# A four-stage convolution kernel: the image loop written out, and the copies of the normalised image dealt to two DMA queues

## The reference

```python
x = x + L0(_gn(x))   # Winograd convolution, tiles of 6 x 6 giving 4 x 4
x = x + L1(_gn(x))   # 3 x 3 convolution to 18 offsets, prelu, then a deformable 3 x 3 convolution:
                     # bilinear samples at the moved places, 8 groups
x = x + L2(_gn(x))   # four 3 x 3 convolutions with binarised weights, quantised activations between
x = x + L3(_gn(x))   # 3 x 3 convolution, |vertical difference| through a 1 x 1, channel attention
```

## Time and profile before

| | |
|---|---|
| median of 3 runs | 4523.1 us |
| profiled execution | 4541.7 us, its span 4539.9 us |
| mean granted clock of TensorE | 0.970 |
| instructions executed | 75043 |
| chain that ended last | PE 70%, DMA 11%, SP's queue 7%, DVE 5%, issue 4%, POOL 2% |
| DMA | 1024 MB, mean 226 GB/s; SP's queue 511.64 MB, ACT's 305.72 MB, POOL's 201.52 MB |

### The profile page before, as it was taken

How to read it: one execution, slowest core, us unless ns; L and a number is a source line. 1 busy time by engine, 2 the same in 40 slices (tenths; PEclk the granted TensorE clock), 3 DMA queues, 4 the chain that set the end, 5 groups by cost and what they waited for, 6 DMA issues and landing times.

```text
span 4539.9 us, 75043 instructions
## 1 busy us (share of the span) xinstructions
PE 4235.0 (93%) x24997; PEld 2030.2 (45%) x24997; DVE 2948.8 (65%) x6076; ACT 1864.5 (41%) x2023; POOL 3088.7 (68%) x3094
## 2 busy tenths in 40 slices
PE   2899999999999999999999999999999999999993
PEld 2444444444444444444444444444444444444441
DVE  5656676666666766677666666766667666766553
ACT  1434444443434434444344434434444344444431
POOL 1777777676776767667677776767767677676750
PEclk8999999999999999999999999999999999999996
DMA  4687788778877787777778877787777777878862
GB/s 112 214 248 228 235 255 231 230 228 237 238 230 233 223 234 237 219 242 234 227 238 244 243 225 232 225 234 240 223 241 234 225 232 232 245 234 235 244 200 61
DMA packets 480356, 1024.07 MB, mean 226 GB/s; under 512 B 262165, under 2 KB 298357, under 8 KB 475637
## 3 DMA queue, kind: packets, MB, share of 16 engines
q1 hardware_dynamic: 324628, 511.64, 39.0%
q10 hardware_dynamic: 57024, 305.72, 20.0%
q0 software_dynamic: 98304, 201.52, 16.2%
HBM read 862.19 MB, written 73.20 MB: 206 GB/s over the span
## 4 chain that ended last, share of the span: by engine, by line
PE 70%; DMA 11%; SPq 7%; DVE 5%; issue 4%; POOL 2%; ACT 0%; ACTq 0%; DVEq 0%; another core or an unknown queue 0%; POOLq 0%
PE ps_r L1512 50%; PE ps_c L1498 6%; DMA taps_c<-plane_act 5%; PE ps_y L1524 5%; DMA plane_act<-act_c 3%; PE ps_a L1451 3%; SPq L434 3%; PE ps_c L1538 2%; POOL ring L622 2%; DMA wino<-patch_table 1%; PE ps_y L1545 1%; SPq L439 1%; PE ps_a L1489 1%; SPq L491 1%; DVE col_hat L1217 1%
## 5 line engine op out<-in xcount | busy, mean ns | idle before, releaser
L622 POOL DMA_INDIRECT ring<-patch_table,idx_part x3072 | 3080.5, 1003 | 1305.1 <-issue 1168.4
L1512 PE MATMUL ps_r<-select,image 128*128 128x512 f32 x6912 | 3183.7, 607 | 59.9 <-issue 48.3
L1512 PEld LDWEIGHTS ps_r<-select,image 128*128 128x128 f32 x6912 | 1270.3, 192 | 1481.8 <-issue 1459.2
L1217 DVE TENSOR_TENSOR col_hat<-ps_r,col_hat 128x512 f32<-128x512 f32 x1152 | 794.8, 690 | 1366.4 <-PE ps_r L1512 1359.0
L672 ACT ACTIVATE select<-row_in,minus_row 128x1536 f32<-128x1536 f32 x384 | 604.1, 1573 | 778.9 <-PE ps_r L1512 731.5
L674 ACT ACTIVATE select<-select,one_col 128x1536 f32<-128x1536 f32 x384 | 605.3, 1576 | 12.5
L691 ACT COPY samples<-ps_c 128x512 f32<-128x512 f32 x256 | 149.8, 585 | 679.1 <-PE ps_c L1538 679.1
L1524 PEld LDWEIGHTS ps_y<-col_hat,w_dense 128*32 128x32 f32 x9216 | 228.7, 109 | 297.1 <-issue 296.2
L1524 PE MATMUL ps_y<-col_hat,w_dense 128*32 128x128 f32 x9216 | 331.9, 277 | 0.0
L1226 DVE TENSOR_TENSOR ps_w<-ring,ps_w 128x384 f32<-128x384 f32 x512 | 284.7, 556 | 31.1 <-DMA ring<-patch_table,idx_part 21.5
L1232 DVE TENSOR_TENSOR ring<-ring,ps_w 128x384 f32<-128x384 f32 x512 | 280.2, 547 | 4.4
(11 more groups left out here) (232 smaller groups left out, 2497.3 us busy)
## 6 DMA issues: line engine op xcount, KB each, us to landing
row_in<-coord_table ACTq DMA_DIRECT2D x384, 768.0 KB
col_hat<-coord_table SPq DMA_DIRECT2D x384, 768.0 KB
ring<-patch_table,idx_part POOLq DMA_INDIRECT x3072
taps_c<-plane_act SPq DMA_DIRECT2D x135, 268.1 KB
taps_c<-xn_c SPq DMA_DIRECT2D x186, 130.0 KB
coord_table<-wino SPq DMA_DIRECT2D x64, 216.0 KB
wino<-xn_a SPq DMA_DIRECT2D x93, 130.0 KB
plane_act<-act_c SPq DMA_DIRECT2D x180, 65.0 KB
```

Source lines behind the costliest of these rows:

```text
L622: nc.gpsimd.indirect_dma_start(out=ring[j][:, h % 2, k, :], out_offset=None, in_=table, in_offset=bass.IndirectOffsetOnAxis(ap=idx_part[:, ...
L1217: v.tensor_tensor(hat_t, ps_r[:, (s + t) % 2], hat_t, ALU.mult).then_inc(tile_weighed, 1)
L1512: ins = mm(ps_r[:, (s + t) % 2], image[:, m, t], select[s % 2][:, m], start=(m == 0), stop=(m == PAIRS - 1))
```

## The change

`schedule` calls `slot` for all periods from -2 to 16 with n a Python number, so nothing is a loop on PE, DVE, ACT and SP any more; `restart` is gone, and an engine's chain semaphore counts on. The 12 copies of the normalised image are shared between SP (even six) and ACT (odd six, at the end of its slot) for every image, in slots 12, 3 and 19. The quantised activations keep their way through the DRAM plane, but for the last image. On PE the offset convolution moves from (14, 2) to (14, 1), and where stages a and c meet in one third, c now comes first.

```diff
     def upto(self, n):
-        self.eng.wait_ge(self.sem, n)
+        if n:
+            self.eng.wait_ge(self.sem, n)
...
-    def restart(self):
-        if self.n:
-            self.join()
-            self.eng.sem_clear(self.sem)
-            self.n = 0
...
 def schedule(eng, chain, slot, prepare=None):
-    def period(n):
+    for n in range(-2, N + 1):
+        if n == 0 and prepare:
+            prepare()
         for s in range(SLOTS):
             slot(n, s)
-    period(-2)
-    period(-1)
-    if prepare:
-        prepare()
-    chain.restart()
-    period(0)
-    chain.restart()
-    with eng.Fori(1, N - 1) as t:
-        period(t)
-        chain.restart()
-    period(N - 1)
-    chain.restart()
-    period(N)
...
-            def copy_taps(dst, src, done, shared):
-                for to, frm in copies(dst, src, range(0, SHIFTS * STRIPS, 2 if shared else 1)):
+            def copy_taps(dst, src, done):
+                for to, frm in copies(dst, src, range(0, SHIFTS * STRIPS, 2)):
                     sp.dma_start(to, frm).then_inc(done, 16)
...
-                    copy_taps(taps_a, xn_a, taps_a_in, first_image(n))
+                    copy_taps(taps_a, xn_a, taps_a_in)
...
-                    copy_taps(taps_c[:], xn_c, taps_c_in, last_image(n))
+                    copy_taps(taps_c[:], xn_c, taps_c_in)
...
-                if s in (6, 9, 12):
+                if s in (6, 9, 12) and last_image(n):
                     act.wait_ge(c_dve.sem, c_dve.at(n, f"relu{(s - 6) // 3}"))
                     share_copies(taps_act, act_c, taps_act_in)
...
-                if first_image(n + 1):
+                if live(n + 1):
                     a_copies(n + 1, s)
-                if last_image(n - 1):
+                if live(n - 1):
                     c_copies(n - 1, s)
...
-                if at == (14, 2):
+                if at == (14, 1):
                     pe.wait_ge(a_dve.sem, a_dve.at(n, "norm1"))
                     pe.wait_ge(taps_a_in, n * COPIES_IN + COPIES_IN)
...
+                    if live(n - 1):
+                        c(n - 1, s, q)
                     if live(n + 1):
                         a(n + 1, s, q)
-                    if live(n - 1):
-                        c(n - 1, s, q)
```

More of the change, by code:

```diff
@@ L403, in copies @@
                 yield dst[dx * C:(dx + 1) * C, lo - dx:hi - dx], src[s * C:(s + 1) * C, lo - s * RS * XW:hi - s * RS * XW]
-        def first_image(n):
-            return known_zero(n)
         def last_image(n):
@@ L548, in c @@
                     if last_image(n):
-                        copy_taps(taps_act, act_c, taps_act_in, True)
+                        copy_taps(taps_act, act_c, taps_act_in)
                     else:
@@ L1253, in gathered_block @@
                     if q == 0:
-                        if s > 0:
-                            chain.upto(summed[0])
+                        chain.upto(summed[0])
                         add_columns(n, g, 1)
@@ L1384, in slot @@
             def slot(n, s):
-                if s == SLOTS - 1 and first_image(n + 1):
+                if s == SLOTS - 1 and known_zero(n + 1):
                     prepare_rest()
```

## The result

| | before | after |
|---|---|---|
| median of the comparison, 4 runs each | 4523.3 us (4519.8 to 4553.5) | 4384.6 us (4381.7 to 4387.1) |
| profiled execution, its span | 4541.7, 4539.9 us | 4387.1, 4385.2 us |
| mean granted clock | 0.970 | 0.983 |
| instructions executed | 75043 | 67257 |

The ratio is 0.968, with a 95% interval of 0.964 to 0.972: faster, by 139 us. Forecast were 4357 us and a range of 4330 to 4456: the side and the range hold, the size is 27 us short.

What follows compares the result with a forecast made beforehand. The prediction took TensorE (PE), busy 93% of the span, as the bound. 71 us for the back edge plus 95 for the copies made 166 off the profiled 4541.7: 4376 profiled, 4357 us median, range 4330 to 4456.

Steps and rivals of the forecast that it cites:

- The sum of 166: Whole forecast gain in us: 71 for writing out the loop plus 95 for dealing the copies.
- the back edge: PE's jump at each image's end: removing 48.3 us of issue waits and 22.4 of slow clock gains 71 us.
- the copies: Slot 12, six copies moved to ACT: store to third convolution falls from 23.97 to 19.7 us, gaining 95 with clock.
- Rival 5: Written-out code pauses elsewhere as long as the jump did, and the copies bring nothing: 4523 us, chance 0.03.
- Moved, not added, 0: PE's offset convolution, one tile earlier, may wait for its own copies; that comes out of the next wait: 0.
- Dealing in slots 3 and 19 at 0: In these slots PE doesn't wait for the copies, so getting them earlier brings 0.
- ACT's issues at 0: Six issues on ACT after each normalisation, bounds 0 and 5.28 us a place: 0, selectors being made a slot ahead.
- Rival 3: Slower by ACT: row_in goes out behind six copies, delaying selectors and PE's transposes; 4602 us, chance 0.05.
- Rival 1: Only the back edge pays, as copies could hold the plane up on two queues too: 4452 us, chance 0.22.
- the page's rule: The skill's statement that starting DMAs on several engines saves only issue time: copies worth 0, sum 71 us.
- Rival 4: POOL's gathers become the bound, a pass can't go under 266 us: 4427 us, chance 0.08.
- Rival 2: Everything clears, both kinds of PE wait and the slow clock: 187 us gained, 4336 us, chance 0.10.

Runs made afterwards that it cites:

- e3: The kernel before with only PE's program written out straight, the other engines keeping the loop: 4444.6 us, ratio 0.980.
- e9: The kernel before with ACT, DVE and SP written out straight and PE alone in the loop: 4515.9 us, ratio 0.997.
- e6: The kernel before with its loop over pairs of images, 7 jumps fewer: 4501.9 us, ratio 0.995.
- e2: The kernel before with all engines written out straight, copies and PE's order unchanged: 4433.5 us, ratio 0.979.
- e10: The kernel before with 64 register moves ahead of PE's loop, meant to shift its code by 4 KB: 4532.4 us, ratio 1.002.
- e11: The kernel before with 128 register moves ahead of PE's loop, meant to shift its code by 8 KB: 4528.5 us, ratio 1.000.
- e1: The kernel before, loop and PE's order kept, with the twelve copies dealt to both queues for every image: 4462.2 us, ratio 0.985.
- e4: The changed kernel with PE's old order, so written out and dealt: 4380.7 us, ratio 0.967.
- e12: The changed kernel without dealing: PE's new order, SP issuing all 12 copies except in the first and last image: 4396.9 us, ratio 0.972.
- e13: e2 with ACT's row_in of slot 15 moved behind its work for stages a and c: 4397.6 us, ratio 0.972.
- e5: The changed kernel with copies dealt in slot 12 alone, SP issuing all 12 in slots 3 and 19 (last image still shared): 4378.0 us, ratio 0.969.
- e7: The changed kernel with all 12 copies of slot 12 on ACT's queue: 4382.0 us, ratio 0.969.

## Why the prediction was right, and what it mis-sized

**The sum's base.** This is 16 of the 27 us. The profiled execution of before was 18.6 us above the median, and I subtracted what its waits and clock showed from the median. Its repeats ran from 4500 to 4554 us and the changed kernel's within 6, so what varies may well stand in the waits that go; no run shows it. Profiled against profiled the forecast was 4376, and 4387 came, 11 us off.

**The sum of 166.** That it came so near is in part luck: against the steps of the experiments (94 us for straight code, then 54 for dealing) the back edge's 71 was 23 us too small and the copies' 95 was 41 too large.

**The back edge, "48.3 + 22.4 clock = 71".** The mechanism is right: the issue waits are gone, PE's code alone brings nearly all of it (e3, 0.980 against 0.979), the others' next to nothing (e9), 3.6 us a jump (e6). As the worth of straight code it was too small: 94 us (e2). The term had only the pause and its own clock. The 34 us of waits for planes that went as well were not seen. Why they went is open: e6 shows that they don't shrink in step with the number of jumps, e10 and e11 failed to move the fetch, and in e2, where it moves by itself, its place matters little. Rival 5 is out, straight code doesn't stall.

**The copies, "23.97 to 19.7, 95 us".** The middle of the two bounds was too cautious for the plane: it has landed 16.9 us behind the store. The 19.5 us to the convolution agree with the 19.7 by chance, for in most passes they are PE's own time. The wait left is 0.4 us a pass against 0.7, held up by three passes of 13. The sum of 95 was worked out beside a loop that still has its waits; alone there the copies brought 70 (e1), on top of straight code 54, and on top of the new order about 20. I added two terms that shared the same plane waits: e1 and e2 alone make 70 + 94 = 164 us, and 148 was measured for the two together (e4, 0.967). With intervals of 15 to 19 us on each, the difference of 16 is within the noise, but the waits for planes show the overlap: e1 takes 51 us off them and e2 34, together 85, and e4 takes off 58.

**"Moved, not added, 0" for the offset convolution.** Right in the changed kernel (e4), wrong as a statement on the order: without dealing it is about 31 us (e12). ACT's row_in, which I never followed there, is held back by it, and that alone gains about as much by the ratios, if less in the traces (e13). The step failed to ask who on ACT waits for PE there, and what that releases.

**Dealing in slots 3 and 19 at 0, ACT's issues at 0.** Both hold (e5; ACT's 184.7 us of waits reach PE for 3.0). Rival 3 had its delay right, six issues of 5.5 us and late row_in; the cover of a slot held.

**Rival 1 and the page's rule.** The plane's path shows store to loads 13.3, 9.9 and 7.8 us with 12, 6 and 0 copies ahead on its queue, the bytes being the same (with 12 and written out, e2, 12.2). Issue time is hardly a part of it: the store goes out 0.1 to 0.4 us behind its activation before and 0.03 us with dealing alone (e1), while the plane lands 5.4 us sooner. So dealing saves more than issue time, against the Trainium skill (DMA: Bandwidth & Descriptors, "Issuing engines are not separate DMA queues") and with a chance of 0.22 given to it. Its point that the engines are shared fits e7, where the loads take as much longer to land as they are issued sooner.

**Rival 4.** POOL's bound of 266 us a pass isn't there: passes take 261.0. **Rival 2** (4336 us) was too good by 49.

**The other 11 us.** From the last image's first row tile to the end the changed kernel takes 354.5 us, before 348.6: 6 us longer, with the 3.02 us at 4088.75 and slow clock behind it. PE's 13 passes, from first row tile to first row tile, take 3392.5 us against 3550.3: 158 us less instead of the forecast's 166, so 8 us short. Ahead of them 3 us were gained.

## What to carry to other kernels

Follow a late transfer by its own queue and by the large transfers that other queues issue within some microseconds of it: holding one 768 KB load back by 8 us was worth 33 us by the ratios, about as much as reordering TensorE's program, and both that order and the dealt copies held it back as a side effect. Terms that remove the same wait don't add, so cost each with the others already in place. Where one engine bounds a hardware loop, write out or unroll that engine's program; a jump cost some 3.6 us here.

## What was not expected of the hardware

Code shifted by 64 or 128 register moves was fetched at the same point of the work, 20 to 22 us behind slot 12's first copy in every pass of e10 and e11 as before. Waits for planes took 58 to 73 us in six kernels that have a loop on at least one engine and undealt copies (e3, e9, e10, e11, e6, before), and 39 us in e2, which has no loop and the same transfers in the same order; a cause for this isn't shown. Behind shorter waits the clock stays up: half clock was 143 us before, 44 in e2, 17 in e12, 24 after and 0 in e5, and PE's busy time for the same instructions is 47 us shorter after, a third of the gain in the two traces. Stacking the held-back row_in on dealt copies wasn't tried.
